# A graph layer's gathers released by another engine: GpSimd waits for VectorE's product in place of TensorE's turning

## What is computed

```python
q = (x @ Wq.T + bq).reshape(N, H, C)          # H, C = 4, 16
k = (x @ Wk.T + bk).reshape(N, H, C)
v = (x @ Wv.T + bv).reshape(N, H, C)
logits = (q[dst] * k[src]).sum(-1) * (1.0 / np.sqrt(C))
m = jax.ops.segment_max(logits, dst, num_segments=N)
e = jnp.exp(logits - m[dst])
denom = jax.ops.segment_sum(e, dst, num_segments=N)
alpha = e / (denom[dst] + 1e-16)
msg = v[src] * alpha[..., None]
out = jax.ops.segment_sum(msg, dst, num_segments=N).reshape(N, HC)
return out + x @ Ws.T + bs
```

## Time and profile before

| | |
|---|---|
| time, median of 3 runs | 3872.41 us (3866.45 to 3875.07) |
| span of the profiled execution | 3819.9 us |
| TensorE busy in the span | 2598.0 us (68%) |
| VectorE busy | 2277.4 us (60%) |
| ScalarE busy | 1404.8 us (37%) |
| GpSimd busy | 1847.1 us (48%) |
| start of the first and of the last gather of line 154 | 197.5 to 2805.1 us |

### The profile page before, as it was taken

One profiled execution on the slowest core, in us unless ns is written; L12 is line 12 of the kernel. 1 busy time (PEld: TensorE's weight loads), 2 busy tenths in 40 slices (PEclk: granted clock), 3 DMA queues, 4 the chain that ended last, 5 costly groups with the idle time before them and its releaser, 6 DMA issues. The chain is left out here.

```text
span 3819.9 us, 47527 instructions
## 1 busy us (share of the span) xinstructions
PE 2598.0 (68%) x13194; PEld 2196.2 (57%) x13194; DVE 2277.4 (60%) x3441; ACT 1404.8 (37%) x2768; POOL 1847.1 (48%) x1956
## 2 busy tenths in 40 slices
PE   2446656666666563466666666666658999999999
PEld 1335445555545453344555445445547999899998
DVE  3236666656766672266666666666655655566655
ACT  6212222222222221022222222222226666676665
POOL 6466666666666646666666666666631000000000
PEclk9755666665566665556666666666658999999999
DMA  9344444434444432344444444444420000000000
GB/s 379 100 102 116 113 112 120 116 110 115 118 112 120 113 93 48 84 110 119 121 123 120 122 119 119 124 114 124 120 76 15 21 5 19 23 11 12 20 10 11
DMA packets 364547, 356.12 MB, mean 93 GB/s; under 512 B 58787, under 2 KB 297682, under 8 KB 364454
## 3 DMA queue, kind: packets, MB, share of 16 engines
q1 hardware_dynamic: 191798, 168.12, 14.0%
q0 software_dynamic: 62832, 125.63, 13.4%
q10 hardware_dynamic: 109824, 61.36, 5.4%
HBM read 246.63 MB, written 108.30 MB: 93 GB/s over the span
## 5 line engine op out<-in xcount | busy, mean ns | idle before, releaser
L154 POOL DMA_INDIRECT kv<-kv_table,ix x1664 | 1582.6, 951 | 842.5 <-issue 468.5
L618 DVE TENSOR_TENSOR_SCAN held_q<-mask,held_q,qT 128x512 f32<-128x512 bf16 x208 | 264.1, 1270 | 785.3 <-remote 733.8
L590 PE MATMUL outT<-identity,run_v 128*128 128x128 f32 x832 | 321.7, 387 | 513.6 <-ACT rows L677 434.1
L568 PE MATMUL kT<-identity,kv 128*128 128x128 f32 x832 | 353.6, 427 | 429.7 <-DMA kv<-kv_table,ix 311.1
L590 PEld LDWEIGHTS outT<-identity,run_v 128*128 128x128 f32 x832 | 219.1, 263 | 573.2 <-ACT rows L677 415.0
L662 ACT ACTIVATE drop<-rise 128x512 f32<-128x512 f32 x208 | 130.9, 629 | 935.6 <-DVE rise L638 478.4
L568 PEld LDWEIGHTS kT<-identity,kv 128*128 128x128 f32 x832 | 193.2, 232 | 446.4 <-issue 375.2
L1245 ACT ACTIVATE full_x<-psH_x,offset_x,scale_x 128x448 f32<-128x448 f32 x448 | 333.6, 745 | 260.3 <-PE psH_x L1098 253.0
L1372 DVE TENSOR_TENSOR hid_lo_x<-full_x,hid_hi_x 128x448 fp32r<-128x448 f32 x448 | 276.1, 623 | 253.4 <-ACT hid_hi_x L1245 242.8
L575 PE MATMUL logit<-kq,head_sum 128*128 128x512 f32 x416 | 389.4, 1039 | 22.6 <-issue 15.8
L592 PE MATMUL restT<-pick,top 128*128 128x8 f32 x1664 | 394.5, 310 | 0.0
(11 more groups left out here) (223 smaller groups left out, 5556.6 us busy)
## 6 DMA issues: line engine op xcount, KB each, us to landing
running_sums<-rows ACTq DMA_DIRECT2D x208, 288.0 KB
qz<-q_at_starts SPq DMA_DIRECT2D x208, 256.0 KB
mask<-masks SPq DMA_DIRECT2D x416, 128.0 KB
q_at_starts<-zeros SPq DMA_DIRECT2D x16, 1664.0 KB
kv<-kv_table,ix POOLq DMA_INDIRECT x1664
x_sb<-in_x SPq DMA_DIRECT2D x1, 6272.0 KB
kv_table<-proj SPq DMA_DIRECT2D x14, 448.0 KB
x_x<-in_x POOLq DMA_DIRECT2D x7, 896.0 KB, 5.7
```

The source lines that it names most:

```text
L154: pool.indirect_dma_start(kv[:, b % UNROLL, j, 2 * HC * s:2 * HC * (s + 1)], None, kv_t, bass.IndirectOffsetOnAxis(ix[:, b, n:n + 1], 0)). ...
L568: pe.transpose(kT[u % 2][:, P * j:P * (j + 1)], kv[:, u, j, 0::2], identity[:, :])
L590: pe.transpose(outT[:, of], run_v[:, u, of], identity[:, :])
L618: dve.tensor_tensor_scan(held_q[:, h, :], mask[:, u, 0, :], qT[:, :], held_q[:, 1 - h, STEP - 1:STEP], ALU.mult, ALU.add).then_inc(q_held, 1)
```

## The change

In the edge phase, on GpSimd's queue, the wait in front of a block's gathers names another semaphore. The count is the same. `weighted` is counted up by VectorE at the end of the product `wv` (line 644), once for each block in both layers, as `v_turned` is by TensorE. The product of a block reads what the turning of that block has written. The order of the instructions on every engine stays as it was.

```diff
                 def _(pool):
                     for b in range(EARLY, BLOCKS):
-                        wait_past(pool, v_turned, BLOCKS * layer + b - U + 1)
+                        wait_past(pool, weighted, BLOCKS * layer + b - U + 1)
                         gather_block(pool, b)
```

## The result

| | before | after |
|---|---|---|
| time, median | 3870.49 us (3866.45 to 3875.07, 4 runs) | 4371.99 us (4361.54 to 4375.91, 4 runs) |
| ratio, 95% interval | | 1.1301 (1.1278 to 1.1323) |
| span of the profiled execution | 3819.9 us | 4365.7 us |

A forecast was written before the change was run, and what follows sets the result against it. GpSimd was taken to pace the edge phases, in a loop of waits with VectorE, at 11.67 us a block. Two countings, +500 and +540 us, gave +520: 3820 + 520 = 4340, plus 52.5 around the span, about 4390 us; range 4050 to 4490.

The forecast's parts named there:

- The new loop: Edge phases: blocks gathered in pairs without a pause inside, 28.7 us a pair, 14.4 us a block against 11.67.
- four terms: Pause before a pair: TensorE's results 3.27 us, VectorE's work 4.80, product 0.68, hand-over 0.2; 8.95 us in sum.
- held_q's long waits: Sign on VectorE: waits of about 10 us or more remain, now in about half of the blocks.
- The rule that the prediction used: When GpSimd issues two blocks without a pause, TensorE's results for the first are seen only after the second is issued.
- The direct shift: GpSimd's wait: product's end plus hand-over less old gather start, mean 2.5 us a block over 200 blocks, +500 us.
- the settled loop: Edge phases: the loop settles into pairs, 2.7 us a block more over 200 blocks, +540 us.
- 52.5 around the span: Time outside the profiled span: median 3872.41 less span 3819.9 us, taken as untouched and added to 4340 us.
- the hold: Edge phases: TensorE's results reach their users only 3.3 to 3.5 us after the second block's last gather was issued.
- Longer pauses that let the results out: Rival: pauses of 1.7 us before every block prevent pairs, 11.4 us a block, -46 us, 3826 us; chance 0.10.
- The rival that hung on GpSimd's wait for TensorE: Rival: removing GpSimd's wait on TensorE's semaphore ends the stall, 10.05 to 10.5 us a block, about 3610 us; chance 0.04.
- the third: Rival: the change does nothing, as something other than line 557 held GpSimd; chance 0.03 for within 0.2%.

The follow-up runs named there:

- a3: The changed kernel, where GpSimd also waits before each block until the previous block's gathers have landed: 4050.74 us, ratio 1.0437 to the kernel before.
- a4: The kernel before, with its old wait, plus a wait before each block until the previous block's gathers have landed: 4050.12 us, ratio 1.0435.
- a1: The kernel before, keeping the wait for `v_turned` and adding the new one for `weighted`: 4388.12 us, ratio 1.1306 to the kernel before.
- a2: The kernel before, its wait moved to the second scan (line 651), 2.4 us behind the product: 4308.45 us, ratio 1.1101 to the kernel before.
- c4: The kernel before, unchanged, run once more on another chip for a second trace: 3460.05 us.

## Why the prediction was right

**The new loop.** Predicted: GpSimd settles into pairs, a pause of 8.95 us in front of every second block. The trace has 99 pauses, 8.8 us in the mean, and 8.82 and 9.08 in the turn shown. Its four terms were 3.27 + 4.80 + 0.68 + 0.2 us and are 3.33 + 4.80 + 0.68 + 0.28. (The 0.2 had been read from two starts that one turning released, which is no hand-over.) A pair is 28.86 us (predicted 28.7), the mean over a phase 14.20 us a block (predicted 14.4): all pairs hold, but in each phase the first three blocks after the one gathered ahead wait for nothing. The idle time before the gathers was predicted at 1360 us and is 1361.9, of which wv ended 873.4 and nearly all the rest is the 0.30 us between gathers. held_q's long waits are in half of the blocks. a3 and a4 show that the pairs with their holds carry the cost, and a1 that waiting for the product makes them. The rule that the prediction used, though, failed for the later wait of a2, and why it held in every pair of the changed kernel is not known: there is luck in how well the terms fit.

**The two terms of the sum.** The direct shift (500 us) and the settled loop (540 us) were two countings of the same thing, and +520 was between them. Counted over all 200 blocks of the trace of before instead of seven, the direct shift is 512 us. Only the second counting describes what the trace after shows; that the first agrees with it isn't explained by any run. Measured in the edge phases: (14.20 - 11.67) x 206 = 521 us.

**What was mis-sized.** The term "52.5 around the span" is shown by no run. In every run that followed, the execution's time is 2 us above its span (c4: 3460.05 against 3458.1; the changed kernel's profiled execution: 4368.07 against 4365.7). The profiled execution of before, whose own time isn't on record, was then one that took some 50 us less than the timed runs; that is inferred, since c4, which was to show it, ran on the chip without the hold. From span to span the change costs 545.8 us. Of these 521 are in the edge phases, 7 in the node phase between them (191.2 against 184.0 us from the last gather of one phase to the first of the next), 15 behind the last gather (1029.0 against 1013.9 us) and 3 ahead of the first; the last three were taken as zero. 4390 came out 18 us from the median since two errors of opposite sign met: the 25 us that weren't in the sum, and the 50 that were added to a span which had none around it. Why one execution of before needs 50 us less isn't settled, nor where the 50 lie; if in the edge phases, a usual execution of before has 11.9 us a block and the change costs 2.3 us a block there and not 2.5.

**The rivals.** Longer pauses that let the results out: the changed wait doesn't bring them about. a3 has longer pauses before every block and no long waits; the price was 12.5 us a block and not 11.4, as a pause there is 2.8 us and not 1.7. Whether the pause alone would do it is open, and 1.7 us is not enough: 8 of 27 blocks before pauses of 1.7 to 2.3 us were held over 6 us in the kernel before. The rival that hung on GpSimd's wait for TensorE is refuted by the changed kernel itself and by a1. Its other half, that a loop without the hold closes at 10.05 us a block, is what c4 shows on another chip. Nothing speaks for the third.

**What the prediction couldn't see.** It took the hold for a property of the kernel. The same kernel ran without it in the last lot of runs, on another chip; with one chip a lot, whether the chip makes the difference, or something else that differed between the lots, isn't shown. Worked out from c4's trace, with a hand-over of 0.2 us, the product of block b-4 would end after block b's present start in 88 of 200 cases, by 37 us in sum. The changed kernel would there take some 37 us more than 3458, about 1%: an estimate, it wasn't run on that chip. The 13% is a number of the lots in which TensorE's results are held (1.1301 and, in a1's lot, 1.1306).

## What to carry to other kernels

When a wait is moved to a later event, don't add the shift to the present timeline only; follow the loop round until it repeats, since a loop with a delay in it can settle in another rhythm. Here both countings came out alike, but only the loop foretold the pauses of 9 us before every second block. Where a rule is only observed, as here, test it at a second point before relying on it: a2 missed by 300 us. Look at the starts of an operation's users, not at its own shown end: a releaser called "remote", and a user that starts 7 to 10 us after what it needs, were the trace of the one stall that mattered. And before tuning against such a stall, run the same kernel again on another chip: here it took 3870 us in three lots of runs and 3458 in the fourth, and the wait that gains 337 us over a1 could only have cost in the fourth.

## What the runs showed of the hardware

- In three of the four lots of runs, VectorE, ScalarE and GpSimd go on late with what TensorE turned while GpSimd makes sixteen indirect DMAs in a row (951 ns each, 0.30 us between). In the changed kernel held_q starts 10.5 to 11.5 us after its keys' turning began where 2.0 us is usual, and 3.0 to 3.4 us after the end of the last of the sixteen; in the kernel before up to 11.6 us, and with a ring of eight blocks up to 17.7 us. The rule isn't strict: 18 pairs of a2 and 5 of a1 have no hold.
- They are not late where GpSimd first waits for its earlier gathers to land (a3, a4, pauses of 2.2 us or more), even while it then makes the next eight; nor while GpSimd fills with no gathers about (698 ns each), nor when SyncE loads the same number of bytes.
- In the fourth lot, on another chip, they are never late, with the same program: 3457.63 against 3870 to 3881 us. From span to span that is 362 us (3819.9 to 3458.1), of which the edge phases have 332 (11.67 and 11.68 against 10.05 and 10.07 us a block). Gathers (953 against 951 ns), instruction counts and HBM bytes are the same; the records of semaphore counts are complete in the fourth lot alone.
- Four more buffers don't shorten the hold; it ends at the same distance behind the run of gathers (3.2 us) and begins earlier.
